# A mixed Mamba and MoE layer on one core: the fourth tile's state sum goes from VectorE to ScalarE and GpSimd

## The reference

```python
def step(h, inp):
    delta_t, B_t, C_t, x_t = inp
    dA = jnp.exp(delta_t[..., None] * A)
    h = h * dA + (delta_t * x_t)[..., None] * B_t[:, None, :]
    y_t = jnp.einsum('bdn,bn->bd', h, C_t)
    return (h, y_t)
```

## The kernel before

| piece | entries of the table | VectorE | GpSimd | ScalarE |
|---|---|---|---|---|
| x0 to x7, convolution | 9 to 16 | L830, three operations, one step later | | two copies out of PSUM |
| ln4 to ln7 | 3, 5, 7, 9 | L838 one step later, L852 two later | L990, L992, two steps later | two logarithm steps |
| ln0 to ln3 | 23, 24, 25, 26 | the same | the same | the same |
| gate0 to gate3 | 21, 22 (two each) | | L999, one step later | |
| silu0, silu1, zsilu0, zsilu1 | 14, 17, 19, 29 | | | table load, 1.9 us, table load, one step later |

## Time and profile before

### The profile page before, as it was taken

How to read it: one execution, slowest core, us unless ns; L and a number is a source line. 1 busy time by engine, 2 the same in 40 slices (tenths; PEclk the granted TensorE clock), 3 DMA queues, 4 the chain that set the end, 5 groups by cost and what they waited for, 6 DMA issues and landing times. The chain is left out here.

```text
span 2029.9 us, 28313 instructions
## 1 busy us (share of the span) xinstructions
PE 1695.2 (84%) x7908; PEld 1258.7 (62%) x7908; DVE 1528.3 (75%) x2037; ACT 793.0 (39%) x1162; POOL 993.6 (49%) x767
## 2 busy tenths in 40 slices
PE   3856777597888888887867779889989999999998
PEld 2344444464445654445444454777878999999997
DVE  0379999999999999999999970477735566556564
ACT  0455555455465465564554431100002233323232
POOL 0067558676478585586776844000004444343343
PEclk9967888699898799897988879899999999999999
DMA  4212211122213222213222243211115666665664
GB/s 101 65 43 59 63 45 48 59 80 79 69 52 104 69 80 86 60 53 110 67 67 64 58 148 112 101 63 62 66 52 128 163 152 140 168 156 136 162 172 66
DMA packets 131939, 184.18 MB, mean 91 GB/s; under 512 B 23313, under 2 KB 81441, under 8 KB 128609
## 3 DMA queue, kind: packets, MB, share of 16 engines
q1 hardware_dynamic: 109200, 132.52, 20.2%
q0 software_dynamic: 17856, 44.85, 11.3%
q10 hardware_dynamic: 4720, 4.86, 0.9%
HBM read 277.64 MB, written 38.15 MB: 156 GB/s over the span
## 5 line engine op out<-in xcount | busy, mean ns | idle before, releaser
L1017 POOL TENSOR_TENSOR arena_kept<-arena_kept,b_all 128x512 f32<-128x512 f32 x512 | 642.0, 1279 | 313.5 <-DVE arena_kept L912 297.5
L912 DVE TENSOR_TENSOR_SCAN arena_kept<-da,arena_kept 128x512 f32<-128x512 f32 x512 | 596.5, 1205 | 19.8 <-ACT da L790 19.8
L790 ACT ACTIVATE da<-arena_kept,a_neg 128x504 f32<-128x504 f32 x512 | 348.5, 685 | 423.5 <-DVE arena_kept L912 419.9
L590 PE MATMUL hT<-ident_kept,arena_kept 128*128 128x128 f32 x2048 | 321.7, 316 | 188.7 <-DVE arena_kept L912 188.2
L590 PEld LDWEIGHTS hT<-ident_kept,arena_kept 128*128 128x128 f32 x2048 | 282.8, 165 | 282.6 <-DVE arena_kept L912 245.5
L925 DVE SCALAR_TENSOR_TENSOR yacc<-hT,c_now,yacc 128x512 f32<-128x512 f32 x480 | 332.7, 734 | 5.5 <-PE hT L590 4.3
L443 PE MATMUL bank<-hid,wt 128*128 128x512 f32 x512 | 259.5, 657 | 26.4 <-ACT arena_kept L646 25.7
L1912 POOL DMA_INDIRECT out<-y,slots_kept x76 | 132.0, 1737 | 258.1 <-issue 186.8
L443 PEld LDWEIGHTS bank<-hid,wt 128*128 128x128 f32 x512 | 104.6, 214 | 142.0 <-issue 113.7
L830 DVE SCALAR_TENSOR_TENSOR arena_kept<-xpad,ch,arena_kept 128x512 f32<-128x512 f32 x96 | 78.5, 817 | 64.5 <-ACT arena_kept L646 62.2
L1780 ACT ACTIVATE gs<-egp 128x352 f32<-128x352 f32 x73 | 33.8, 463 | 235.8 <-PE eup L1112 227.4
(11 more groups left out here) (214 smaller groups left out, 3110.3 us busy)
## 6 DMA issues: line engine op xcount, KB each, us to landing
w_up_kept<-in_up_T SPq DMA_DIRECT2D x76, 1408.0 KB, 6.1
w_dn_kept<-in_dn_T SPq DMA_DIRECT2D x76, 768.0 KB, 7.4
b_all<-bt_scratch SPq DMA_DIRECT2D x128, 256.0 KB, 3.5
wt<-in_in_T SPq DMA_DIRECT2D x64, 256.0 KB, 3.0
wt<-in_out_T SPq DMA_DIRECT2D x32, 256.0 KB, 2.9
x_in<-in_x_pad ACTq DMA_DIRECT2D x16, 256.0 KB
res<-in_x_pad SPq DMA_DIRECT2D x16, 256.0 KB, 4.5
x_scratch<-res SPq DMA_DIRECT2D x16, 256.0 KB, 2.0
```

The source lines that it names most:

```text
L590: mm = nc.tensor.transpose(hT[t][:, d * P:(d + 1) * P], h[:, m % RING, d, t * P:(t + 1) * P], ident[:])
L790: nc.scalar.activation(out[:, :, 1:], rows[:, :, 1:], ACT.Exp, scale=a_neg[:, d, n:n + 1]) \
L912: nc.vector.tensor_tensor_scan(h[:, n % RING, i, :], da[i % RING][:], dbx[:, i, :], 0.0, ALU.mult, ALU.add).then_inc(scan_done, 1)
L1017: nc.gpsimd.tensor_tensor(dbx[:, i, :], u[:, d, :], b_all[:, m % RING, :], ALU.mult) \
```

## The change

Of each half, for states 0 to 13, tile 3 is no longer summed by VectorE. ScalarE multiplies hT3 by C and writes the product to SBUF: for state 0 to yacc itself, for states 1 to 13 to a new buffer `stage`. GpSimd then adds `stage` to yacc[3]. States 14 and 15 stay with VectorE. ScalarE does this for state m-2 in step m, behind its second decay; GpSimd in step m behind its four `inflow` and ahead of its pieces. TensorE waits for ScalarE's copy where it waited for VectorE's sum before it transposes into hT3 again. The first scan of a step now waits for the transposes of the step two before. `xam`, a buffer of the adapter piece, moves into x2_sb[1] to make room.

```diff
+SHIFTED = (3,)
+SHIFTED_STATES = NST - 2
...
+    xam = x2_sb[:, 1, :]
+    stage = sb("stage", [P, len(SHIFTED), HT * P])
...
             def turn_h(j, m, tiles):
                 pe.wait_ge(scan_done, j * SCANS + SCAN0 + HT * (m + 1))
+                last = (j, m - 1) if m else (j - 1, STEPS - 1)
                 for t in tiles:
-                    pe.wait_ge(sum_done, j * SUMS + TB * m + t + 1)
+                    if last[0] >= 0 and shifted(last[1], t):
+                        pe.wait_ge(scaled[t], scaled_by_act(*last))
+                    elif last[0] >= 0:
+                        pe.wait_ge(sum_done, sums_by_dve(*last, t))
...
+            def scale_state(j, m, t):
+                n = m % NST
+                act.wait_ge(hT_full, j * SUMS + TB * m + t + 1)
+                if n == 0:
+                    act.wait_ge(c_copied, j + 1)
+                    if m or j:
+                        act.wait_ge(bank_full, Place("body", j, "turn0" if m else "turn1").uses[-1].number + 1)
+                    out = yacc[:, t, :]
+                else:
+                    act.wait_ge(added[t], ADDED * (added_states(j, m) - 1))
+                    out = stage[:, SHIFTED.index(t), :]
+                nc.scalar.mul(out, hT[t][:], c_now[:, t, n:n + 1]).then_inc(scaled[t], 1)
...
                         decay(j, *divmod(m, NST), i)
+                        for t in SHIFTED:
+                            if m >= 2 and shifted(m - 2, t) and i == t - SHIFTED[0] + 1:
+                                scale_state(j, m - 2, t)
...
+                if i == 0 and j * SUMS + TB * (m - 1) > 0:
+                    dve.wait_ge(hT_full, j * SUMS + TB * (m - 1))
                 dve.wait_ge(da_full, at + 1)
...
             def add_state(j, g, n, t):
+                m = g * NST + n
+                if shifted(m, t):
+                    return
...
+            def add_shifted(j, m, t):
+                pool.wait_ge(scaled[t], scaled_by_act(j, m))
+                nc.gpsimd.tensor_tensor(yacc[:, t, :], yacc[:, t, :], stage[:, SHIFTED.index(t), :], ALU.add).then_inc(added[t], ADDED)
...
                     for i in range(HT):
                         inflow(j, *divmod(m, NST), i)
+                    for t in SHIFTED:
+                        if m >= 2 and (m - 2) % NST and shifted(m - 2, t):
+                            add_shifted(j, m - 2, t)
```

More of the change, by code:

```diff
@@ L157, in __init__, with shifted, sums_by_dve, scaled_by_act @@
                 self.dve = use.place
+SHIFTED = (3,)
+SHIFTED_STATES = NST - 2
+def shifted(m, t):
+    return t in SHIFTED and m % NST < SHIFTED_STATES
+def sums_by_dve(j, m, t):
+    own = [(k, tile) for k in range(STEPS) for tile in range(TB) if not shifted(k, tile)]
+    return j * len(own) + sum(at <= (m, t) for at in own)
+def scaled_by_act(j, m):
+    return j * HALVES * SHIFTED_STATES + m // NST * SHIFTED_STATES + min(m % NST + 1, SHIFTED_STATES)
+def added_states(j, m):
+    return scaled_by_act(j, m) - (j * HALVES + m // NST + 1)
 def turned_bc(block):
@@ L234, in mamba @@
     x1T = sb("x1T", [P, KM, BLK])
-    xam = sb("xam", [NADAPT * LRANK, BLK])
     x2T = sb("x2T", [P, KM, BLK])
@@ L297, in mamba @@
     sum_done = sem("sum_done")
+    scaled = {t: sem(f"scaled{t}") for t in SHIFTED}
+    added = {t: sem(f"state_added{t}") for t in SHIFTED}
     c_copied = sem("c_copied")
     y_ready = [sem(f"y_ready{half}") for half in range(HALVES)]
-    DBX0, SCAN0, SUM0 = RING * HT, HT, TB
+    DBX0, SCAN0 = RING * HT, HT
+    ADDED = 1
     SKIP0, Y0 = 1, HT
@@ L485, in turn @@
             def turn(at, half):
-                pe.wait_ge(sum_done, at.block * SUMS + SUM0 + (0 if half else SUMS // HALVES))
+                pe.wait_ge(sum_done, sums_by_dve(at.block - 1, STEPS - 1, TB - 1) if half else sums_by_dve(at.block, NST - 1, TB - 1))
                 for d in range(HT):
@@ L535, in mixed @@
                 pe.wait_ge(dve_emptied, Place(section, j, "xa").dve + 1)
-                nc.tensor.matmul(bank[:], b_T[:, e * P:(e + 1) * P], xam[:], start=False, stop=True).then_inc(bank_full, 1)
+                nc.tensor.matmul(bank[:], b_T[:, e * P:(e + 1) * P], xam, start=False, stop=True).then_inc(bank_full, 1)
             def x2_row(section, j, at, t):
@@ L869, in masked @@
                 dve.wait_ge(mask_step, 2)
+                dve.wait_ge(x2_stored[1], 16 * TB // RING * b)
                 dve.wait_ge(bank_full, at.full + 1)
-                nc.vector.tensor_tensor(xam[:].rearrange("p (b l) -> p b l", b=BB), banks[at.bank][:].rearrange("p (b l) -> p b l", b=BB),
+                nc.vector.tensor_tensor(xam.rearrange("p (b l) -> p b l", b=BB), banks[at.bank][:].rearrange("p (b l) -> p b l", b=BB),
                                         mask[:, b * BB:(b + 1) * BB].unsqueeze(2).broadcast_to([P, BB, SEQ]),
@@ L915, in add_state @@
             def add_state(j, g, n, t):
-                at = j * SUMS + TB * (g * NST + n) + t
+                m = g * NST + n
+                if shifted(m, t):
+                    return
                 scalar = c_now[:, t, n:n + 1]
-                dve.wait_ge(hT_full, at + 1)
+                dve.wait_ge(hT_full, j * SUMS + TB * m + t + 1)
                 if n == 0:
@@ L923, in add_state @@
                 else:
-                    dve.wait_ge(sum_done, at + SUM0 - TB + 1)
+                    if shifted(m - 1, t):
+                        dve.wait_ge(added[t], ADDED * added_states(j, m - 1))
+                    else:
+                        dve.wait_ge(sum_done, sums_by_dve(j, m - 1, t))
                     nc.vector.scalar_tensor_tensor(out=yacc[:, t, :], in0=hT[t][:], scalar=scalar, in1=yacc[:, t, :],
@@ L928, in _ @@
             dve.sem_inc(scan_done, SCAN0)
-            dve.sem_inc(sum_done, SUM0)
             for s in range(RING):
@@ L941, in _ @@
                 dve.wait_ge(dve_emptied, turned_bc(j).dve + 1)
-                dve.wait_ge(sum_done, j * SUMS + SUM0)
+                if j:
+                    dve.wait_ge(sum_done, sums_by_dve(j - 1, STEPS - 1, TB - 1))
+                    for t in SHIFTED:
+                        dve.wait_ge(scaled[t], scaled_by_act(j - 1, STEPS - 1))
                 nc.vector.tensor_copy(c_now[:], c_next[:]).then_inc(c_copied, 1)
```

## The result

| kernel | median, us | profiled execution, its span | ratio to before, 95% interval |
|---|---|---|---|
| before, run beside it | 2028.14 | 2031.67, 2029.9 | |
| changed | 2045.22 | 2043.21, 2041.4 | 1.0075 [1.0059, 1.0092] |

The change makes the kernel slower by 0.75%, 15 us. The ratio leaves out one of the changed kernel's four executions, a slow one of 2267.39 us at a granted clock of 0.724 where the others show 0.90. The medians lie 17 us apart and the spans 11.5; the 4 to 6 us between these figures lie in the spread of single executions (17 executions of before, run beside gap24, go from 2024.9 to 2036.4 us). The forecast was 2032 with a range of 2000 to 2050 for it and its rivals together: 2045 lies in that, but outside the 2022 to 2042 that it gave itself.

What follows compares the result with a forecast made beforehand. VectorE was taken to bound the scan stage. Losses of 79.4 us against 72.8 gained gave +6.6 on the 2029.9 us span, 2032 carried to the median; own range 2022 to 2042, with rivals 2000 to 2050.

Steps and rivals of the forecast that it cites:

- one-operation steps 4 to 9 (all), 10 and 11 (block 3): Steps with one piece operation: it waits for GpSimd's last inflow, losing 16.9 us; 2 us taken back in steps 5, 7, 9.
- convolution, steps 10 to 14: Blocks 0 to 2: three piece operations wait out inflow and add, 25.2 us lost; step 10's extra operation and pair, 2.0.
- steps 15 to 17: Step 17, three blocks: no add follows, only the first wait, 2.0 us lost; steps 15 and 16 keep all sums.
- steps 22 to 28, blocks 0 to 2: GpSimd falls behind through adds, gates and pairs; VectorE waits at step 24; 7.75 us lost a block, 23.3 for three.
- steps 22 to 28, block 3: The same steps in the last block, which has only the gates: 1.8 us lost.
- behind a silu: Steps 18, 20 and 30: VectorE already waits for ScalarE, so the wait grows by the removed sum, 7.2 us in all.
- late b_all, step 3: Blocks 1 to 3: step 4's inflow starts late when b_all lands; the scan waits about 1.0 us, 3 us in all.
- The turns: VectorE operations with two SBUF inputs and GpSimd operations never run together; the later waits until about 0.13 us before the other's end.
- E: The moment in a step when VectorE can go on behind the fourth scan; the forecast counts its times from it.
- GpSimd becomes the bound: Rival, steps 22 to 31 and behind step 4: GpSimd's lag is carried on; about 2063 us, half of it 2047; chance 0.23.
- The gain mostly stays: Rival: fewer meetings of VectorE and GpSimd, gain of 55, 1970 us, or about 2000 with half the losses; chance 0.24.
- Late hand-over: Rival: TensorE stands waiting for ScalarE's product and pieces come late, 24 us in steps with two heavy pieces, 2056; chance 0.08.

Runs made afterwards that it cites:

- gap24: Changed kernel with one more GpSimd wait per block (0 to 2), for its own last add, just ahead of step 24's inflow: 2034.28 us, ratio 1.0023.
- no_add: Changed kernel without GpSimd's 104 adds and the waits for them, the fourth tile's sum left out: 2003.22 us, ratio 0.9864.
- bench_long: Bench without the layer: GpSimd runs n products unbroken before VectorE asks with two SBUF inputs, six more ready: 1.07 us for n to 12, 7.17 from 16.
- gates_late: Changed kernel with GpSimd's four gates moved from steps 22 and 23 to steps 28 to 31: 2029.72 us, ratio 0.9998.
- free_steps: Changed kernel with the hand-over only where no piece with two SBUF inputs follows, and the gates in steps 28 to 31: 2015.39 us, ratio 0.9933.
- add_ready: Changed kernel with all sums given back to VectorE and an unread GpSimd addition at each of the 104 places: 2054.14 us, ratio 1.0123.

## Why the prediction was right in kind and short in size

The difference of the two traces can be put into the prediction's own terms, from the first scan of each of the 128 steps (a step's growth, plus 0.65 us where a sum was moved, is what was lost there):

| term | forecast, us | measured, us |
|---|---|---|
| one-operation steps 4 to 9 (all), 10 and 11 (block 3) | 16.9 - 2.0 | 13.8 |
| convolution, steps 10 to 14 | 25.2 + 2.0 | 23.7 |
| steps 15 to 17 | 2.0 | -2.2 |
| steps 22 to 28, blocks 0 to 2 | 23.3 | 33.9 |
| steps 22 to 28, block 3 | 1.8 | 3.8 |
| behind a silu | 7.2 | 8.8 |
| late b_all, step 3 | 3.0 | 2.6 |
| sum lost | 79.4 | 84.4 |
| gained, 112 x 0.65 | 72.8 | 72.8 |
| net | +6.6 | +11.6 |

**What held.** The removed sum is worth 0.65 us (steps 1, 2, 19, 21, 29: 0.65 to 0.66). The turns hold wherever GpSimd's run is short, and they eat the gain in every step with a piece. At 461.17 us L902 of a one-operation step took 1.59 us, and its step was 0.2 us shorter than before, as reckoned:

```profile
461.17 1.59 DVE L902 TENSOR_TENSOR arena_kept<-arena_kept 128x512 f32<-128x512 f32 x1
```

Step 24's inflow came late by 1.64, 1.67 and 1.63 us in blocks 1 to 3 (forecast 1.7) and by 0.94 in block 0. The b_all of step 4 came late by 1.00 us in block 1 (forecast 1.0 in each of blocks 1 to 3; block 2 shows 1.38 and block 3 none, so the sum of 2.6 is in part chance). In block 1 it is the scan's wait and the inflow's:

```profile
431.20 2.43 DVE L965 TENSOR_TENSOR_SCAN arena_kept<-da,arena_kept 128x512 f32<-128x512 f32 x2 [1.00 <-POOL arena_kept L1077]
...
429.79 4.98 POOL L1077 TENSOR_TENSOR arena_kept<-arena_kept,b_all 128x512 f32<-128x512 f32 x4 [3.97 <-DMA b_all<-bt_scratch]
```

**What was mis-sized.** The term "steps 22 to 28". The prediction walked GpSimd's queue rightly to the point where it has no gap from step 21 on, and then let VectorE have its turn at step 24 after at most one instruction. That last step is the one that failed. With an unbroken run of 22 it waits out all that stand ready: 4.83 instead of some 1.3 us, 3.5 a block, 10.5 in all. gap24 took just this away and gave 11 us back; its steps 22 to 28 of blocks 0 to 2 lose 22.8 us where the forecast had 23.3. With it the kernel stands at +0.23%, inside the 0.5% that the forecast had named as the likeliest outcome. Turns are the rule of the trace before because no such run occurs there ahead of a piece (8 instructions at most); nothing in it spoke for more.

**What was smaller.** The convolution steps and steps 15 to 17 came 8 us better. The add starts at E+1.5, not 1.6, and the second and third operations fit behind it: 3.91 us from 508.75, the next scan at 512.57, 4.46 behind E (508.11) where I had 4.62. Steps 15 and 17 came out shorter than reckoned, which I didn't follow up. It is luck that these errors go against the one above: without them the sum would have missed by 13 us instead of 5.

**The rivals.** "GpSimd becomes the bound" had the right place (steps 22 to 31) and nearly the right time (2047), but by another mechanism: its price was the meeting of single operations with the add and longer pairs, and the one-operation steps came out no worse than forecast. "The gain mostly stays" is out: even with no adds on GpSimd at all 46 of the 72.8 us are lost. "Late hand-over" is out by no_add and by TensorE's few waits for ScalarE.

The Trainium skill (SBUF — State Buffer, Who interferes with whom) has the shared pair held for a whole instruction and the other side blocked until then. Up to the 13th instruction of a run the traces agree; the 4.83 us and bench_long's 7.17 go beyond it.

**What stays open.** Why the count matters, and where between the 13th and the 16th instruction it turns. Also open is the part of the 15 us that the two traces do not show.

## What to carry to other kernels

Giving GpSimd elementwise work beside a VectorE that reads two operands from SBUF is paid in turns: list, step by step, which of VectorE's operations will meet it, and move work only into steps without them; with the gates late in both, that turned 0.9998 (gates_late) into 0.9933 (free_steps) here. Watch for the place where the added work closes GpSimd's last gaps. If an instruction of VectorE shows several GpSimd instructions under it at full length, break GpSimd's run with one wait for its own instruction just before, or spread its side work. A wait that was met long ago is not enough: the inflow's waits for the scan in the run of 22 left no gap.

## What the runs showed of the hardware

- A VectorE operation with two SBUF inputs that asked during the 16th or a later instruction of a GpSimd run without a gap stayed out until the run ended: 7.17 us with six 128x512 products ready, for n = 16 to 28; during the 13th or an earlier one it got in at the next end, 1.07 us. Instructions count, not their length, and a wait on the instruction just before sets it back.
- A wait named after the last semaphore of several can hide the real one: 11 waits of VectorE named TensorE; 8 belonged to ScalarE's decay and 3 to GpSimd's inflow.
- 104 GpSimd additions that nobody waits for made the kernel 22 to 25 us longer (ratios 1.0110 and 1.0123); the one profiled execution of add_ready shows 15.6 us of it.
